# Where the scanned rows are asked for in the last stage of a four-layer image kernel

## The chip, the cores and the metric

The kernel runs on one core of one Trainium2 chip. The metric is the device time of one execution in microseconds (us). The profile comes from one further execution, taken by the hardware profiler on the same kernel.

## What is computed

The program applies four residual layers to 8 images of 256 x 256 x 64 floats. Only the last step of the last layer matters here. The fourth layer sees each image as a table of 4096 points with 256 channels; 1024 of these points are masked. For the masked points a sequential scan over the 1024 points gives new rows; these replace the old rows in the table, and the table is added to the image:

```python
def step(prev, inp):
    mn, bst, mx = inp
    ...
    cur = (d_ad[:, None] * prev + mx[:, None] * bst) / (d_ad + mx + EPS)[:, None]
    return (cur, cur)
_, gen = jax.lax.scan(step, jnp.zeros((b, c), x.dtype), xs)
out = feats.at[:, :, mask_point_idx].set(gen.transpose(1, 2, 0))
return out.reshape(b, c, h, w)
...
x = x + _L3_conv_ref(_gn(x), ...)
```

## The kernel before

The stages run one behind the other, each a block with its own programs for the five engines and a barrier at its end. The scan (`coherent_scan`) writes its rows to a tensor in device memory, `gen`, for all 8 images together; it ends at 14875 us of the profile. The change is in the stage behind it, the last one, `finish_points` (lines 2089 to 2180 or so). It goes through the images b = 0 to 7, and has five programs:

- SyncE (SP) issues all loads, in the order of its code, on one DMA queue (q1 in the profile). For each image: the scanned rows `g` (line 2116, 1024 rows of 1 KB, 1 MB in all), then the table of all points `f` (line 2120, 4096 rows of 1 KB, 4 MB), then the input `x` in two halves (line 2125, 2 MB each, runs of 8 KB). `g` has two buffers, used in turn, and so has `f`. Each half of `x` has one.
- GpSimd (POOL) writes the scanned rows of the image into the table `ft` in device memory, with eight indirect DMAs of 128 rows each (line 2133, queue q0). It waits for `g` of the image and for the row numbers.
- VectorE (DVE) makes the row numbers of the next image (lines 2158 to 2160). There is one set of them, so it first waits until the eight indirect DMAs of this image are done (semaphore `s_sc`). Then it makes 16 additions (line 2169), each of the transposed table in PSUM and a piece of `x`. Both are in this order in the code: the row numbers of image b+1 are written ahead of the additions of image b, behind those of image b-1.
- TensorE (PE) transposes the table, 64 blocks of 128 x 128 for an image (line 2147), once `f` has landed. It is ahead of the additions by at most four of the PSUM tiles.
- ScalarE (ACT) only issues the stores of the result, 2 MB for each half image (line 2178, queue q10), each once its eight additions are done.

SP's load of `f` for image b has to wait until the indirect DMAs of image b are done (they write what it reads), and for b of 2 and more until the table two images back is transposed. SP's load of a half of `x` waits for the eight additions of that half of the image before. The load of `g` for image b waits, from b = 2 on, for the indirect DMAs of image b-2, whose buffer it takes. Since SP works through its list in order, a wait in front of one load holds all later ones.

Of the kernel before, what the change touches and what calls it, by code (L numbers as in the profile page):

```python
# [14 lines left out]
P = 128  # L15
# [2073 lines left out]
def finish_points(nc, B, x3, ft, gen, mask_idx, eye, out):  # L2089

    TM, NT = NMASK // P, NPTS // P
    with ExitStack() as ctx:
        m = Mem(nc, ctx, "fp")
        g = m.sb("g", [P, 2, TM, H])
        f = m.sb("f", [P, 2, NT, H])
        x = m.sb("x", [P, 2, 2, NPTS // 2])
        o = m.sb("o", [P, 2, 2, NPTS // 2])
        idx0, idx, idxf = m.sb("idx0", [P, TM], I32), m.sb("idx", [P, TM], I32), m.sb("idxf", [P, TM])
        idn = m.sb("idn", [P, P])
        tp = [m.ps(f"tp{i}", [P, 2, 2, P]) for i in range(4)]  # L2100
        s_const, s_idx, s_ch = m.sem("const"), m.sem("idx"), m.sem("ch")
        s_g, s_f, s_x = ([m.sem(f"{n}{j}") for j in range(2)] for n in ("g", "f", "x"))
        s_sc, s_t, s_o = m.sem("sc"), m.sem("t"), m.sem("o")
        s_store = [m.sem(f"store{j}") for j in range(2)]
        ftf = ft.rearrange("b n h -> (b n) h")
        HT = NT // 2
        with nc.Block() as block:  # L2107

            @block.sync
            def _(sp):  # L2110
                sp.dma_start(idn[:, :], eye).then_inc(s_const, 16)  # L2111
                sp.dma_start(idx0[:, :], mask_idx.rearrange("(t p) -> p t", p=P), allow_slow_non_contiguous=True).then_inc(s_const, 16)  # L2112
                for b in range(B):
                    if b >= 2:
                        sp.wait_ge(s_sc, 16 * TM * (b - 1))
                    sp.dma_start(g[:, b % 2, :, :], gen[b].rearrange("(t p) h -> p t h", p=P)).then_inc(s_g[b % 2], 16)
                    sp.wait_ge(s_sc, 16 * TM * (b + 1))
                    if b >= 2:
                        sp.wait_ge(s_t, (b - 1) * HT)
                    sp.dma_start(f[:, b % 2, :, :], ft[b].rearrange("(t p) h -> p t h", p=P)).then_inc(s_f[b % 2], 16)  # L2120
                    for q in range(2):
                        if b:
                            sp.wait_ge(s_o, ((b - 1) * 2 + q + 1) * (HT // 2))
                        c0 = q * (NPTS // C // 2)
                        sp.dma_start(x[:, q, :, :], x3[b, :, c0:c0 + NPTS // C // 2, :].rearrange("(r p) w c -> p r (w c)", p=P)).then_inc(s_x[q], 16)  # L2125

            @block.gpsimd
            def _(pool):
                for b in range(B):
                    pool.wait_ge(s_g[b % 2], 16 * (b // 2 + 1))  # L2130
                    pool.wait_ge(s_idx, b + 1)
                    for i in range(TM):
                        pool.indirect_dma_start(ftf, bass.IndirectOffsetOnAxis(ap=idx[:, i:i + 1], axis=0),  # L2133
                                                g[:, b % 2, i, :], None).then_inc(s_sc, 16)

            @block.tensor
            def _(pe):
                pe.wait_ge(s_const, 32)
                for b in range(B):
                    pe.wait_ge(s_f[b % 2], 16 * (b // 2 + 1))  # L2140
                    for k in range(HT):
                        n = b * HT + k
                        if n >= 4:
                            pe.wait_ge(s_o, n - 3)
                        for r in range(2):
                            for i in range(2):
                                last = nc.tensor.transpose(tp[n % 4][:, r, i, :], f[:, b % 2, 2 * k + i, r * P:(r + 1) * P], idn[:, :])  # L2147
                        last.then_inc(s_t, 1)

            @block.vector  # L2150
            def _(dve):
                ch = Chain(dve, s_ch)
                dve.wait_ge(s_const, 32)
                ch.step(nc.vector.tensor_copy(idxf[:, :], idx0[:, :]))
                nc.vector.tensor_copy(idx[:, :], idxf[:, :]).then_inc(s_idx, 1)
                for b in range(B):
                    if b + 1 < B:
                        ch.step(nc.vector.tensor_scalar(idxf[:, :], idxf[:, :], float(NPTS), None, ALU.add))
                        dve.wait_ge(s_sc, 16 * TM * (b + 1))  # L2159
                        nc.vector.tensor_copy(idx[:, :], idxf[:, :]).then_inc(s_idx, 1)  # L2160
                    for k in range(HT):
                        n, q = b * HT + k, k // (HT // 2)
                        dve.wait_ge(s_t, n + 1)
                        if k % (HT // 2) == 0:
                            dve.wait_ge(s_x[q], 16 * (b + 1))
                            if b:
                                dve.wait_ge(s_store[q], 16 * b)  # L2167
                        c0 = (k % (HT // 2)) * 2 * P
                        nc.vector.tensor_tensor(o[:, q, :, c0:c0 + 2 * P], tp[n % 4][:, :, :, :].rearrange("p r i n -> p r (i n)"),  # L2169
                                                x[:, q, :, c0:c0 + 2 * P], ALU.add).then_inc(s_o, 1)  # L2170

            @block.scalar
            def _(act):
                for b in range(B):
                    for q in range(2):
                        act.wait_ge(s_o, (b * 2 + q + 1) * (HT // 2))
                        c0 = q * (NPTS // C // 2)
                        act.dma_start(out[b, :, c0:c0 + NPTS // C // 2, :].rearrange("(r p) w c -> p r (w c)", p=P),
                                      o[:, q, :, :]).then_inc(s_store[q], 16)
                for q in range(2):  # L2180
                    act.wait_ge(s_store[q], 16 * B)
# [671 lines left out]
```

## Time and profile before

| | us |
|---|---|
| median of 3 runs | 15209.85 |
| lowest and highest | 15209.34, 15213.14 |
| span of the profiled execution | 15214.5 |
| last stage in it, from its first load (14875) to the end | 339 |

The page of the profile gives the span from the first to the last instruction of one execution. No time around that span is given for this execution; the span itself is 4.65 us above the median of the three timed runs. Over the whole span TensorE's matrix work is busy 66%, VectorE 61%, ScalarE 52%, GpSimd 34%; the last 2.2% of the span, the stage of the change, is the part in which the DMA engines are busiest. To read it, one cuts this stage out of the trace: its chain of waits, the busy share and rate of the DMA engines in short stretches, and the share of each DMA queue.

### The profile page before, as it was taken

Reading aid. Unit: us, or ns where it says so; the run is one execution under the profiler, and the core shown is the slowest. Engines: PE = TensorE matmul, PEld = TensorE weight load, DVE = VectorE, ACT = ScalarE, POOL = GpSimd, SP = SyncE. Lnnn points to the kernel's source line nnn. Section 1 sums busy time; section 2 is a strip of 40 time slices with the busy share of each in tenths; the row PEclk is TensorE's granted clock in tenths of the full one; section 3 lists DMA queues with packets and bytes.
Section 4 is the critical chain, followed back from the end, with each engine's and each line's share of the span. In section 5 each row is a group of like instructions: output and inputs, shape, how many; then the busy total and the mean of one; then the engine's idle time right before and its main releaser. Section 6 shows DMA issues by size and latency. Waiting matters only on the chain. (4 is left out here: it accounts for less than half of the span.)

```text
span 15214.5 us, 295101 instructions
## 1 busy us (share of the span) xinstructions
PE 9980.4 (66%) x105986; PEld 7080.0 (47%) x105986; DVE 9300.2 (61%) x20130; ACT 7945.1 (52%) x14451; POOL 5137.7 (34%) x3844
## 2 busy tenths in 40 slices
PE   8655657999999998778777799866846770000002
PEld 3253223777777776666666688623223330000002
DVE  3213435777777777888888533225444547888882
ACT  5211223777777776566666422352334436777770
POOL 0003334556555555333333355300007891000001
PEclk9878878999999999999999999997878885555555
DMA  6787674111111111011111399978996661000008
GB/s 252 197 171 216 213 233 156 42 42 42 40 41 41 42 42 58 28 67 45 67 45 67 138 364 363 328 264 310 376 386 226 206 205 42 12 12 12 12 12 310
DMA packets 1245925, 2176.95 MB, mean 143 GB/s; under 512 B 99573, under 2 KB 900997, under 8 KB 1177605
## 3 DMA queue, kind: packets, MB, share of 16 engines
q1 hardware_dynamic: 813156, 1637.88, 32.9%
q10 hardware_dynamic: 410912, 463.54, 8.6%
q0 software_dynamic: 20608, 58.22, 1.5%
q8 instruction: 864, 14.16, 0.4%
q14 instruction: 385, 3.15, 0.1%
HBM read 1369.30 MB, written 790.14 MB: 142 GB/s over the span
## 5 line engine op out<-in xcount | busy, mean ns | idle before, releaser
L781 POOL TENSOR_TENSOR la_s<-la_s,la_mx 128x512 f32<-128x512 f32 x2048 | 2093.0, 1043 | 1462.7 <-DVE la_mx L740 1462.3
L2147 PE MATMUL fp_tp<-fp_idn,fp_f 128*128 128x128 f32 x512 | 89.6, 348 | 2547.0 <-DMA fp_f<-ft 2529.7
L820 ACT ACTIVATE la_et<-la_pt 128x512 f32<-128x512 f32 x2048 | 1119.0, 598 | 732.2 <-PE la_pt L652 732.1
L652 PE MATMUL la_pt<-la_idn,la_s 128*128 128x128 f32 x8192 | 1164.5, 287 | 220.5 <-POOL la_s L781 219.8
L2147 PEld LDWEIGHTS fp_tp<-fp_idn,fp_f 128*128 128x128 f32 x512 | 79.9, 184 | 2557.3 <-issue 2340.8
L740 DVE TENSOR_REDUCE la_mx<-la_s 128x16 f32<-128x1024 f32 x1024 | 1243.2, 1214 | 17.7
L732 DVE TENSOR_TENSOR la_s<-la_ps,la_post 128x2048 f32<-128x2048 f32 x512 | 1167.9, 2281 | 27.9 <-PE la_ps L638 27.7
L652 PEld LDWEIGHTS la_pt<-la_idn,la_s 128*128 128x128 f32 x8192 | 913.5, 145 | 334.2 <-issue 231.8
L1439 PE MATMUL pj_pp<-pj_pw,pj_at 128*128 128x256 f32 x4096 | 926.4, 379 | 0.0
L2133 POOL DMA_INDIRECT ft<-fp_g,fp_idx x64 | 62.2, 971 | 2503.4 <-DMA fp_g<-gen 2486.3
L956 PE MATMUL gm_xp<-gm_fws,gm_y 128*128 128x258 f32 x2048 | 559.7, 420 | 421.8 <-ACT gm_ri L1040 421.8
L1913 PE MATMUL sp_cp<-sp_tc 128*128 128x512 f32 x1536 | 697.1, 615 | 168.5 <-ACT sp_cos L1879 162.2
L1439 PEld LDWEIGHTS pj_pp<-pj_pw,pj_at 128*128 128x128 f32 x4096 | 758.3, 190 | 92.7
L1472 ACT ACTIVATE pj_at<-pj_tp 128x512 f32<-128x512 f32 x512 | 277.9, 594 | 861.0 <-PE pj_tp L1429 861.0
L2418 DVE SCALAR_TENSOR_TENSOR i_xo<-i_fp,i_xr 128x256 f32<-128x256 f32 x1024 | 379.8, 419 | 539.5 <-PE i_fp L2325 347.6
L1797 POOL DMA_INDIRECT sp_rows<-ft,sp_idx x256 | 242.8, 949 | 1339.6 <-DVE sp_idx L1922 1253.8
L1511 DVE TENSOR_TENSOR pj_o<-pj_pp,pj_xl 128x256 f32<-128x256 f32 x512 | 215.3, 420 | 753.1 <-PE pj_pp L1439 753.1
L956 PEld LDWEIGHTS gm_xp<-gm_fws,gm_y 128*128 128x128 f32 x2048 | 401.7, 206 | 563.5 <-issue 476.2
L2473 ACT ACTIVATE i_sq<-i_xo 128x4096 f32<-128x4096 f32 x64 | 231.5, 3617 | 814.4 <-issue 593.4
L1326 POOL TENSOR_TENSOR gm_sr<-gm_pc 128x512 f32<-128x512 f32 x64 | 70.0, 1093 | 1697.0 <-DVE gm_pc L1274 1697.0
L2440 POOL TENSOR_TENSOR i_acc<-i_acc,i_xo 128x4096 f32<-128x4096 f32 x56 | 496.3, 8862 | 410.9 <-DVE i_xo L2418 409.7
L751 DVE RECIPROCAL la_rc<-la_pt 128x32 f32<-128x32 f32 x512 | 183.2, 358 | 728.0 <-PE la_pt L661 728.0
(298 smaller groups left out, 28104.7 us busy)
## 6 DMA issues: line engine op xcount, KB each, us to landing
f_xt<-in_x SPq DMA_DIRECT2D x128, 1024.0 KB, 8.0
i_xr<-in_x SPq DMA_DIRECT2D x64, 2048.0 KB, 9.1
x<-pj_o SPq DMA_DIRECT2D x64, 2048.0 KB, 10.2
f_xt<-x SPq DMA_DIRECT2D x128, 1024.0 KB, 14.1
i_xr<-x SPq DMA_DIRECT2D x64, 2048.0 KB, 14.6
x<-i_xo ACTq DMA_DIRECT2D x64, 2048.0 KB, 14.5
sp_xt<-x SPq DMA_DIRECT2D x144, 512.0 KB, 4.6
out<-sp_xt SPq DMA_DIRECT2D x144, 512.0 KB, 2.9
```

The lines of the kernel that those rows point to most:

```text
L652: last = nc.tensor.transpose(t_bank(S, i)[:, h, :], s[:, S % RS, i, h, :], idn[:, :])
L732: nc.vector.tensor_tensor(s[:, S % RS].rearrange("p t h i -> p h t i"), ps[:, :, :, :, :, :].rearrange("p h g e d i -> p h (g e) (d i)"), ...
L740: nc.vector.reduce_max(mx[:, S % RS, ts, :].rearrange("p t h -> p (t h)"), s[:, S % RS, ts].rearrange("p t h (d i) -> p (t h d) i", d=2), ...
L781: nc.gpsimd.tensor_tensor(sv, sv, mb, ALU.subtract).then_inc(s_sub, 1)
L820: nc.scalar.activation(et[:, k % RT].rearrange("p h n -> p (h n)"), t_bank(S, i)[:, :, :].rearrange("p h n -> p (h n)"), ACT.Exp).then_inc ...
L956: last = nc.tensor.matmul(xp[c % 2][q][:, :], y[:, c % 2, wh, q * P:(q + 1) * P], fws[:, q, wh, :], start=(wh == 0), stop=(wh == 1))
L1439: last = nc.tensor.matmul(pp[gg // 2][:, gg % 2, :, :].rearrange("p w d -> p (w d)"), at[:, q, s, g * P:(g + 1) * P], pw[:, s, :, :].rearr ...
L1472: last = nc.scalar.activation(at[:, k % 2, s, :], tp[k % 2][s][:, :], ACT.Copy)
L1797: pool.indirect_dma_start(rows[:, b % 2, i, :], None, ftf, bass.IndirectOffsetOnAxis(ap=idx[:, i:i + 1], axis=0)).then_inc(s_g[b % 2][i // ...
L1913: last = nc.tensor.matmul(cp[n % 4][:, :], tc[:, r, i * P:(i + 1) * P], tc[:, r, c0:c0 + 512], start=(r == 0), stop=(r == 1))
L2418: last = nc.vector.scalar_tensor_tensor(halves(xo, j, r, i)[:, s], f[:, s], 0.0, x[:, s], ALU.max, ALU.add)
L2440: nc.gpsimd.tensor_tensor(acc[:, :], acc[:, :], xo[:, wc % 2, :], ALU.add).then_inc(s_acc, 1)
```

## The change

SP now issues the scanned rows of images 0 and 1 at once, directly behind the two small constants. Those of image b+2 are issued directly behind the table of image b, ahead of the two halves of the input. The wait in front of `g` is gone as a line of its own: the wait in front of the table of image b (all indirect DMAs up to image b done) stands ahead of it and covers it, since `g` of b+2 takes the buffer of `g` of b. No other engine's program is touched.

```diff
+                def rows(b):
+                    sp.dma_start(g[:, b % 2, :, :], gen[b].rearrange("(t p) h -> p t h", p=P)).then_inc(s_g[b % 2], 16)
+
+                rows(0)
+                rows(1)
                 for b in range(B):
-                    if b >= 2:
-                        sp.wait_ge(s_sc, 16 * TM * (b - 1))
-                    sp.dma_start(g[:, b % 2, :, :], gen[b].rearrange("(t p) h -> p t h", p=P)).then_inc(s_g[b % 2], 16)
                     sp.wait_ge(s_sc, 16 * TM * (b + 1))
                     if b >= 2:
                         sp.wait_ge(s_t, (b - 1) * HT)
                     sp.dma_start(f[:, b % 2, :, :], ft[b].rearrange("(t p) h -> p t h", p=P)).then_inc(s_f[b % 2], 16)
+                    if b + 2 < B:
+                        rows(b + 2)
                     for q in range(2):
```

At the start of the stage, SP's queue holds before (`fp_g` is the scanned rows, `fp_f` the table, `fp_x` the input, a closing x2 stands for two loads alike; the numbers behind L are lines of each kernel):

```order
1082 L2112 DMA fp_idx<-in_L_conv_mask_point_idx 128x8x1
1083 L2116 DMA fp_g<-gen 128x8x256
1084 L2120 DMA fp_f<-ft 128x32x256
1085 L2125 DMA fp_x<-x 128x2x2048 x2
1086 L2116 DMA fp_g<-gen 128x8x256
1087 L2120 DMA fp_f<-ft 128x32x256
1088 L2125 DMA fp_x<-x 128x2x2048 x2
```

The same place of SP's queue now:

```order
1082 L2112 DMA fp_idx<-in_L_conv_mask_point_idx 128x8x1
1083 L2114 DMA fp_g<-gen 128x8x256 x2
1084 L2122 DMA fp_f<-ft 128x32x256
1085 L2114 DMA fp_g<-gen 128x8x256
1086 L2129 DMA fp_x<-x 128x2x2048 x2
1087 L2122 DMA fp_f<-ft 128x32x256
1088 L2114 DMA fp_g<-gen 128x8x256
```

The rows of image 1 moved from behind the input of image 0 to in front of the table of image 0, and those of image 2 from behind the input of image 1 to in front of the input of image 0. At the end of the stage SP's queue holds before, for images 6 and 7:

```order
1101 L2116 DMA fp_g<-gen 128x8x256
1102 L2120 DMA fp_f<-ft 128x32x256
1103 L2125 DMA fp_x<-x 128x2x2048 x2
1104 L2116 DMA fp_g<-gen 128x8x256
1105 L2120 DMA fp_f<-ft 128x32x256
1106 L2125 DMA fp_x<-x 128x2x2048 x2
```

and now, for images 5 (its input) to 7:

```order
1101 L2129 DMA fp_x<-x 128x2x2048 x2
1102 L2122 DMA fp_f<-ft 128x32x256
1103 L2129 DMA fp_x<-x 128x2x2048 x2
1104 L2122 DMA fp_f<-ft 128x32x256
1105 L2129 DMA fp_x<-x 128x2x2048 x2
```

Between the input of image 6 and the table of image 7 no load stands any more.

## Rows read from the trace of the kernel before

**Rows 1.** Waits, 14800 to 15215 us: who waited for what, us, times, longest.
```profile
POOL ft L2133 <- DMA fp_g<-gen: 2486.3, 8, 2272.8
DVE fp_o L2169 <- DMA fp_x<-x: 170.8, 8, 30.3
...
SPq L2120 <- DMA ft<-fp_g,fp_idx: 223.2, 8, 29.8
```

**Rows 2.** Chain that ended last, one image: start us, duration us, what.
```profile
14893.17 0.37 SPq L2120
...
14893.58 8.62 SPq L2125
...
14903.46 17.76 DMA fp_g<-gen
...
14921.49 0.97 POOL ft L2133
...
14930.42 3.26 DMA ft<-fp_g,fp_idx
...
14933.69 0.37 SPq L2120
```

**Rows 3.** Stretches: length, busy of the engines, then TensorE clock, DMA share, GB/s.
```profile
14882.00:14893.00 11.00, 0.00 (x0) 0.00 (x0) 0.00 (x0) 0.00 (x0) 7.57 (x8) 0.50 0.27 95
...
14900.00:14905.00 5.00, 0.00 (x0) 0.00 (x0) 0.00 (x0) 0.00 (x0) 0.00 (x0) 0.50 1.10 348
14908.00:14913.00 5.00, 3.65 (x16) 3.28 (x16) 0.00 (x0) 0.00 (x0) 0.00 (x0) 0.50 1.01 419
...
14925.00:14930.00 5.00, 0.00 (x0) 0.00 (x0) 0.00 (x0) 0.00 (x0) 3.78 (x5) 0.50 1.01 398
14930.00:14935.00 5.00, 0.00 (x0) 0.00 (x0) 0.17 (x1) 0.00 (x0) 1.08 (x2) 0.50 0.64 216
14935.00:14940.00 5.00, 0.00 (x0) 0.00 (x0) 0.00 (x0) 0.00 (x0) 0.00 (x0) 0.50 1.00 335
...
15095.00:15100.00 5.00, 0.00 (x0) 0.00 (x0) 0.17 (x1) 0.00 (x0) 0.00 (x0) 0.50 0.64 195
...
15205.00:15210.00 5.00, 0.12 (x2) 0.00 (x0) 1.80 (x4) 0.00 (x0) 0.00 (x0) 0.80 1.01 418
14893.00:15201.00 308.00, 85.44 (x480) 76.34 (x481) 74.80 (x132) 0.00 (x0) 54.35 (x56) 0.61 0.98 361
8800.00:9600.00 800.00, 800.00 (x4438) 714.66 (x4437) 261.93 (x739) 199.98 (x369) 430.11 (x184) 1.00 1.05 363
...
11200.00:11400.00 200.00, 50.79 (x280) 46.10 (x278) 99.18 (x84) 46.79 (x69) 0.00 (x0) 0.61 1.03 412
```

**Rows 4.** DMA issues, 14870 to 15215 us: count, KB each, median us to landing.
```profile
fp_f<-ft SPq DMA_DIRECT2D x8, 4096.0 KB, 15.3
fp_x<-x SPq DMA_DIRECT2D x16, 2048.0 KB, 18.0
out<-fp_o ACTq DMA_DIRECT2D x16, 2048.0 KB
fp_g<-gen SPq DMA_DIRECT2D x8, 1024.0 KB, 17.8
ft<-fp_g,fp_idx POOLq DMA_INDIRECT x64, 4.6
```

**Rows 5.** DMA queues, 15045 to 15050 us: packets, MB, share of 16 engines.
```profile
q10 hardware_dynamic: 228, 1.74, 85.3%
q0 software_dynamic: 93, 0.26, 13.9%
```

**Rows 6.** Timeline: start us, duration us, engine, line, operation, count.
```profile
14881.76 1.00 POOL L2133 DMA_INDIRECT ft<-fp_g,fp_idx  x1 [2272.80 <-DMA fp_g<-gen]
...
15176.69 0.37 SPq L2120 DMA_DIRECT2D fp_f<-ft  x1
...
15201.32 5.47 DVE L2169 TENSOR_TENSOR fp_o<-fp_tp,fp_x 128x512 f32<-128x512 f32 x9 [0.16 <-PE fp_tp L2147]
```

## The prediction

> **What bounds the kernel now.** The change touches only the last stage, 339 us of 15214.5, so nothing outside it can move, and the most that the stage can give is small. I read it in this order. First the waits: GpSimd waits for the scanned rows before every image (the 2486.3 us hold 2272.8 us ahead of the stage, so 213.5 us fall inside it, over 8 images), VectorE waits 170.8 us for the input, and SP waits 223.2 us for the indirect DMAs before it may ask for a table [rows 1]. Every compute engine waits for data. Then the chain of one image: SP issues the table at 14893.17 and the first half of the input right behind, an issue that takes 8.62 us; then it asks for the rows of the next image at 14903.46, which take 17.76 us to land, because they stand in one queue behind 8 MB of table and input. Only then do the eight indirect DMAs start (14921.49), the last one is issued at 14930.42 and lands 3.26 us later, and at 14933.69 SP issues the next table [rows 2]. So by the chain the period of an image is issue, rows, indirect writes, issue: 14933.69 - 14893.17 = 40.5 us. The same period holds to the end: the eighth table is issued at 15176.69 [rows 6], and (15176.69 - 14893.17) / 7 = 40.50 us.
>
> Read alone, this chain promises far too much: 17.8 us of waiting for rows in each image would seem to go. The third view corrects it. The DMA engines are busy 0.98 of the time from 14893 to 15201, at 361 GB/s, and almost without a break: 1.10, 1.01, 1.01 in the stretches with table, input, and stores beside indirect writes; only where one image hands over to the next does the share fall, to 0.64 in 14930 to 14935, and to 0.64 in 15095 to 15100 [rows 3]. **The stage is bound by its bytes**; the chain is late only because its transfers stand behind other bytes that have to be moved anyway. What the change can take is the hole at the handover, plus what it moves into an idle time.
>
> **The size of the hole.** Two ways. By the share: 0.36 x 5 us = 1.8 us of full idleness in each of the two stretches named [rows 3]. That is a lower end, since the ramp on either side is cut off (the next stretch, 14935 to 14940, moves 335 GB/s instead of 348). By the bytes: an image moves 4096 KB of table, 1024 KB of rows and 1024 KB of indirect writes (8 x 128 rows of 1 KB), all in runs of 1 KB, and 4096 KB of input and 4096 KB of stores in runs of 8 KB [rows 4]. The 1 KB runs went at 348 GB/s (14900 to 14905), input alone at 419, stores alone at 418 [rows 3]. So 6.29 MB / 348 = 18.1 us and 8.39 MB / 418.5 = 20.0 us, together 38.1 us: the floor of a period. 40.5 - 38.1 = 2.4 us of hole. That the costs may be added like this shows in 14925 to 14930, where stores run beside indirect writes at 398 GB/s, between the two rates. I take 2.2 us, between the two ends.
>
> **The change part by part.** (a) Rows of image b+2 behind the table of image b, seven handovers. SP issues the same number of loads. Rows of image b+2 are in SBUF long before they are used. What then releases the indirect writes of b+2 is VectorE, whose row numbers come behind the additions of image b: the same moment in an image as now (the first is issued at 14921.49, [rows 2], as the additions end), but one image earlier for the same data. Let L be the time when the last half of input b lands. The additions end about 5 us later (nine of them took 5.47 us, [rows 6]); the indirect writes of b+2 run from L+5, and at today's pace (14921.49 to 14933.69, 12.2 us) end at about L+17. The table of b+2 has to stand in SP's queue before the bytes of image b+1 run out, at L+38.1. The slack is 21 us. The table of b+1 already stands behind the input of b when this lands, so at the handover there is work in the queue, and the hole goes: 7 x 2.2 = 15.4 us (ends 7 x 1.8 = 12.6 and 7 x 2.4 = 16.8). What is late next is nothing on an engine but the bytes, 38.1 to 38.3 us for an image. The input is pushed back by 1 MB of rows in its own image, 3.0 us at 348 GB/s, but the same 3.0 us no longer stand behind it, so the sum of bytes doesn't change; the first image shows it as a later addition, and no later one does.
>
> (b) Rows of image 1 ahead of the first table. They now move while the first eight indirect writes are being made, when the DMA engines are busy 0.27 of the time (14882 to 14893, [rows 3]). 1.05 MB / 348 = 3.0 us leave the saturated part. This cover has 11 x 0.73 = 8 us of room, so it is fully hidden. Indirect writes of image 1 likewise begin at about 14893 instead of 14921, but their bytes stay in the saturated part: nothing.
>
> (c) The rows of image 0 now share the engines with those of image 1. They are first in the same queue; at best they land as now, at worst all of the 3.0 us later. The queue takes requests in order ([rows 2]: rows behind 8 MB landed behind them), so I take 0.5 us, ends 0 and 3.0.
>
> (d) The removed wait and the order of buffers: nothing was queued on it, the wait of the table stands there already.
>
> (e) The tail. From the landing of the last input to the end nothing changes: nine additions from 15201.32, then the last store [rows 6]. Both kernels pay it.
>
> **Does mixing cost?** Before, table and input ran alone, and stores ran beside rows and indirect writes. Now stores of image b (8 KB runs on their own queue) run beside the table of b+1 (1 KB runs). No stretch of this stage shows that pair. The nearest rows: 8800 to 9600, loads and stores mixed in runs of mostly 1 KB, 363 GB/s; 11200 to 11400, stores in 1 KB runs beside loads in longer ones, 412 GB/s [rows 3]. With 363 for all 1 KB runs the period is 17.3 + 20.0 = 37.3 us, a further 0.8 us, 5 us in the stage; the other end is a loss of the same size. I take none, as the nearest row to this pair is the 398 of stores beside indirect writes.
>
> Sum: 15.4 + 3.0 - 0.5 = 17.9 us. On the profiled execution: 15214.5 - 17.9 = 15196.6. The median of the timed runs is 4.65 us below this span, so 15209.85 - 17.9 = **15192.0 us**.
>
> **How the queues share.** The one thing that is in danger is the pace of the indirect writes, which now meet two other queues. Beside stores they got 0.26 MB in 5 us, 52 GB/s, against 1.74 MB of stores [rows 5], though GpSimd issues 1 MB in about 10 us, some 100 GB/s; they caught up after the stores. So they are already held back by a queue of long runs. The Trainium skill says in "DMA: Bandwidth & Descriptors", section "Queues, rings and completion order", that each DMA engine serves its queues in turn, a packet at a time; by that rule the short packets get less than an equal share beside long ones, and the trace agrees in direction. The sum doesn't use the rule; the third rival is what it would do if it hit harder.
>
> **Rivals.**
> 1. Rates mix better than they add. 412 GB/s in 11200 to 11400 is for about a quarter of the bytes in 1 KB runs; if 1 KB runs went at 390 beside stores, the period would be 16.1 + 20.0 = 36.1 us, and the stage would gain 7 x 4.4 + 3.0 - 0.5 = 33 us: 15177. Against it: the stores take most of the engines while they last, and most of the table then runs alone, at 348. Chance 0.07.
> 2. The handover stays a bound, or the memory behind it does: a period of 40 us or a little more whatever the order, since the mean rate over an image can't rise above 361 GB/s [rows 3]. Then only part (b) and a remainder are left, 3 to 8 us: about 15204. For it: 363 GB/s in 8800 to 9600, with the DMA engines never idle. Against it: 419, 398 and 418 GB/s in stretches of this stage and 412 over 200 us elsewhere. Chance 0.11. The Trainium skill states in "DMA: Bandwidth & Descriptors", section "Specifications", a limit of about 358 GB/s from device memory for a core; by that 14.68 MB would need 41.0 us for an image, and the change would bring nothing. The trace speaks against that page, with 419 GB/s of input read from device memory.
> 3. Slower: indirect writes starved. In 15045 to 15050 they had 52 GB/s against one queue of 8 KB runs. If two such queues halved it to 26 GB/s for the whole of an image, 1.05 MB would take 40 us from L+5, the table of the next image but one would be issued at L+45 and begin about 1.7 us later: a period of 47 us, 6 us above today's for six images, less 3: about +33 us, 15243. It decides from the point at which the writes take more than 33 us (38.1 - 5); up to that they cost nothing. Against it: long runs of both queues meet only late in the period, when the input is under way; right behind the additions the load queue holds the table in 1 KB runs. Chance 0.04.
> 4. The change doesn't do what it says: some row load is still held, for instance because SP, in order, stands in the 8.62 us issue of an input [rows 2], and the table of b+1 comes into the queue too late in some images. It would leave half of the holes: gain 10 us, 15200, inside the range. Chance 0.08.
>
> **How the numbers follow.** The forecast (15183 to 15198) has 0.70. The range reaches from the gain with 1 KB runs at 363 and the larger hole, 7 x 3.2 + 3.0 = 25.4, and half of rival 1 (about 15178), to most of rival 2 (15205): 15178 to 15205. 0.2% of this time is 30.4 us, about what a measurement of this kernel can tell from no change. A gain of more needs a period under 36.6 us: only rival 1 with the upper end of everything, 0.06. A loss of more needs rival 3: 0.04. Within 0.2%: 0.90.
>
> **What would show it.** In the profile of the changed kernel: tables (line 2122) no longer one per 40.5 us but with inputs landing, and additions beginning, every 38 to 38.5 us; the DMA share at about 1.0 in every 5 us stretch from 14895 to about 15180, no stretch below 0.9; GpSimd waiting for VectorE's row numbers and no longer for rows, from image 2 on; the wait of SP for the indirect DMAs near zero from image 1 on, its time now in issues and in the wait for additions; the chain through table and input. Part (b) shows as a DMA share of about 0.5 instead of 0.27 in 14882 to 14893. Part (c) as the first indirect write later than 14881.76 [rows 6]. Wrong would be: 5 us stretches without holes but with a rate under 380 GB/s on the mean (rival 2), indirect writes that take over 30 us (rival 3), or a table issued after the input before it has landed (rival 4).

## The result

| | kernel before | changed kernel |
|---|---|---|
| median of 21 runs each, us | 15210.39 | 15181.89 |
| lowest and highest | 15199.65, 15224.01 | 15168.75, 15197.00 |
| span of the profiled execution | 15214.5 | 15167.1 |
| last stage in that profile, from its first load to the end | 339.3 | 310.8 |

The ratio is 0.9981, with a 95% interval of 0.9974 to 0.9987: 28.5 us less, 0.19%. The forecast was 17.9 us less (15192.0), range 15178 to 15205. Sign, range and the class "within 0.2%" held; the size was a third too small, and the inner interval of the forecast, 15183 to 15198, was missed by 1 us.

The profiled span alone would say 47 us. It must not be read so: the last stage begins at 14856.28 in the changed kernel and at 14875.17 before, though nothing ahead of it was touched. That is the spread of the earlier stages from execution to execution. The stage is what the change can move, and it became 339.33 - 310.82 = 28.5 us shorter, which is what the medians say. All experiments below are therefore compared by the length of the last stage.

**The profile after.** Stretches of the last stage of the changed kernel; the last three columns are TensorE's clock, the share of the DMA engines and GB/s:

```profile
14863.00:14874.00 11.00, 0.00 (x0) 0.00 (x0) 0.00 (x0) 0.00 (x0) 7.82 (x8) 0.50 0.45 155
14895.00:14900.00 5.00, 1.18 (x6) 0.77 (x4) 0.00 (x0) 0.00 (x0) 0.00 (x0) 0.84 1.01 423
14915.00:14920.00 5.00, 0.00 (x0) 0.00 (x0) 0.00 (x0) 0.00 (x0) 3.78 (x5) 0.50 1.04 431
14925.00:14930.00 5.00, 0.73 (x4) 0.73 (x5) 0.00 (x0) 0.00 (x0) 0.00 (x0) 0.50 1.10 368
14930.00:14935.00 5.00, 2.94 (x14) 2.54 (x12) 0.00 (x0) 0.00 (x0) 0.00 (x0) 0.50 1.05 425
...
14890.00:15150.00 260.00, 85.19 (x464) 79.72 (x464) 71.48 (x125) 0.00 (x0) 46.54 (x48) 0.61 1.05 400
```

The last line is the mean over most of the stage. The handover hole of [rows 3] is gone, and the mean rate rose from 361 to 400 GB/s. (The stage was not the part of the kernel with the busiest DMA engines, as the section on the profile before has it: 8800 to 9600 has a share of 1.05, this stage had 0.98 [rows 3].) The stretch of the first indirect writes, 0.27 before, is at 0.45: the rows of image 1 run there.

The waits in the same stage, by engine and then those of SP (us in all, times, longest):

```profile
POOL ft L2137 <- DMA fp_g<-gen: 2273.8, 1, 2273.8
DVE fp_o L2173 <- DMA fp_x<-x: 200.6, 8, 26.5
POOL ft L2137 <- DVE fp_idx L2164: 163.3, 7, 27.1
```

```profile
SPq L2129 <- DVE fp_o L2173: 37.9, 2, 20.2
...
SPq L2122 <- DMA ft<-fp_g,fp_idx: 19.5, 2, 16.4
```

Against [rows 1]: GpSimd waits for rows only before the first image, and then for VectorE's row numbers. SP waits 19.5 us for indirect writes, nearly all ahead of the first table, where it waited 223.2. VectorE waits for the input for longer than before, 200.6 us against 170.8, although the kernel is faster: the wait did not go, it became a wait for bytes alone.

One image in SP's queue, from its chain (start, duration; 2114 rows, 2129 input, 2122 table):

```profile
14890.36 0.70 SPq L2122
...
14891.11 31.37 SPq L2114
...
14922.52 3.58 SPq L2129
...
14926.14 0.82 SPq L2129
...
14927.08 0.54 SPq L2122
```

The tables of images 1 to 7 are issued from 14890.36 to 15110.84, so a period is 220.48 / 6 = 36.75 us, against 40.50 before and 38.3 in the forecast. The issue of the rows takes 31.37 us: table and rows now stand behind the input of the image before, and SP stands in the issue until 14922.48. That it waits there for room in its queue is inferred; no run tries it. It costs nothing, since the table issued at 14890.36 takes about 39 us to land (38.8 in the median), so SP is free about 7 us before the table has drained.

### The profile page after: what moved, and what is told of

It is laid out like the page before. It is cut to its first block and busy times, and to the rows that moved or that the text cites. A ratio compares the mean times of both kernels' runs of the same rounds, so it can differ in the third digit from the quotient of the medians.

```text
span 15167.1 us, 295101 instructions
## 1 busy us (share of the span) xinstructions
PE 9973.6 (66%) x105986; PEld 7082.3 (47%) x105986; DVE 9285.7 (61%) x20130; ACT 7946.3 (52%) x14451; POOL 5138.4 (34%) x3844
```

## The experiments

Each kernel is compared by its last stage. The stage repeats well: 339.3 and 339.2 us for the kernel before, 310.8 and 311.1 for the changed one (each in two profiles), while single total times moved by 10 us and more. The period is the time from the issue of the third table to that of the eighth, over 5; by it the kernel before has 40.4 and the changed one 36.8.

| kernel | stage, us | period, us | against |
|---|---|---|---|
| before, again | 339.2 | 40.5 | |
| rows of images 0 and 1 only | 333.1 | 40.6 | before: -6.2 |
| rows one image ahead | 331.1 | 39.3 | before: -8.1 |
| table on two queues (from before) | 369.8 | 44.2 | before: +30.6 |
| stores on the load queue | 312.8 | 37.2 | changed: +1.9 |
| rows in runs of 8 KB | 306.7 | 36.3 | changed: -4.3 |
| table and rows in long runs | 301.6 | 35.0 | changed: -9.3 |
| first input early | 304.4 | 36.2 | changed: -6.5 |
| long runs and early input | 297.7 | 35.0 | changed: -13.3 |
| table in runs of 4 KB | 303.8 | 35.1 | changed: -7.2 |
| 4 KB runs and early input | 302.8 | 35.1 | changed: -8.2 |
| changed, again | 311.1 | 36.6 | |

**The yardstick.**

> The kernel before once more. The last stage, from SP's first load in it to the end of the span, took 339.3 us in the profile before. Every theory here is about this stage alone; if its length is the same to 1 us while the whole span moves by several us, the stage length is the finer measure and the earlier stages are the noise. Expected: 338 to 341 us.

Measured: stage 339.2 us; total 15196.25 us, against 15206.82 for the same program beside it. The stage is the finer measure.

> The changed kernel once more, for the repeatability of its stage: 310.8 us in its profile; expected 310 to 312 us. If it comes out more than 1.5 us away, the differences of 2 us in the other runs say nothing.

Measured: 311.1 us. Differences of 2 us can be read.

**Part (b) alone.** In the changed kernel, the rows of later images go back behind the input:

```diff
                     sp.dma_start(f[:, b % 2, :, :], ft[b]...
-                    if b + 2 < B:
-                        rows(b + 2)
                     for q in range(2):
                         ...
+                    if 1 <= b < B - 1:
+                        rows(b + 1)
```

> Part (b) alone: the rows of images 0 and 1 are asked for at once, those of every later image stay behind the whole input of the image before (their old place). My sum: 3.0 us for the bytes moved into the idle time, and one handover (image 0 to 1) without a hole, 2.2 to 3.7 us; the other six periods stay at 40.5 us. Stage 333 to 335 us. Rival, that the early start of the first indirect writes is what speeds up the whole stage (a better phase between queues that then stays): later periods at 37 to 38 us and a stage under 322 us.

Measured: 333.1 us. Of the stage's 28.3 us (means of the two profiles of each kernel), 6.2 come from the start and the first handover; the other 22.1 us are six handovers of 3.7 us. So part (b) with (c) is 6.2 - 3.7 = 2.5 us, the forecast's 3.0 - 0.5, and the later periods are as before: an early start does not speed up the rest.

**One image ahead instead of two.**

```diff
                 rows(0)
-                rows(1)
...
-                    if b + 2 < B:
-                        rows(b + 2)
+                    if b + 1 < B:
+                        rows(b + 1)
```

> The rows of image b+1, not b+2, directly behind the table of image b; image 0 alone first. Theory that it is enough to have the rows before the handover: the rows land beside the table, about 20 us into a period, the indirect writes of b+1 take 12 to 15 us and are done by 35 us of 37: period 37 to 38, stage 312 to 320 us (310.8 plus 3 for the first rows). Rival, that indirect writes beside loads in 8 KB runs are slowed to 26 GB/s or so (1 MB in 40 us): the table of b+1 comes late, period over 42 us, stage over 345 us.

Measured: 331.1 us, period 39.3: between the two, and neither as it was put. The stretches at a handover of this kernel:

```profile
14990.00:14995.00 5.00, 5.00 (x29) 4.80 (x27) 3.32 (x7) 0.00 (x0) 2.71 (x3) 0.61 0.96 390
14998.00:15003.00 5.00, 0.04 (x1) 0.00 (x0) 1.97 (x5) 0.00 (x0) 0.00 (x0) 0.77 0.97 270
```

The first indirect write was issued at 14983.40, as the rows had landed, and the eight ran until 14995.59 beside the last input, and the table was issued just then, as the input had landed (14994.85). A hole stays, at 270 GB/s, partly filled by the store. The writes were not slowed to 26 GB/s: 12.2 us from the first issue to the next table, the same as before the change. The 40 us of my third rival do not come about; the rows simply came too late, 26.8 us into the period (14956.62 to 14983.40) and not the 20 of the expectation. That is what the second buffer of rows is for: two images ahead closes the hole, one does not.

**Is 348 GB/s a limit of one queue?** In the kernel before, the second half of each table is loaded from ACT's queue:

```diff
-                    sp.dma_start(f[:, b % 2, :, :], ft[b].rearrange(...)).then_inc(s_f[b % 2], 16)
+                    sp.dma_start(f[:, b % 2, :HT, :], ft[b, :NPTS // 2].rearrange(...)).then_inc(s_f[b % 2], 16)
...
             @block.tensor
-                    pe.wait_ge(s_f[b % 2], 16 * (b // 2 + 1))
+                    pe.wait_ge(s_f[b % 2], 32 * (b // 2 + 1))
...
             @block.scalar
                 for b in range(B):
+                    act.wait_ge(s_sc, 16 * TM * (b + 1))
+                    if b >= 2:
+                        act.wait_ge(s_t, (b - 1) * HT)
+                    act.dma_start(f[:, b % 2, HT:, :], ft[b, NPTS // 2:].rearrange(...)).then_inc(s_f[b % 2], 16)
```

> The kernel before, but the second half of each table is loaded from ACT's queue instead of SP's, at the same point. Same bytes, same runs of 1 KB, same waits. Theory that one queue of 1 KB runs by itself does not use the DMA engines fully (348 GB/s) and that a second queue beside it fills them: the table moves at 380 to 400 GB/s, 1.0 to 1.6 us less per image, stage 327 to 332 us. Rival, that 348 GB/s is what 1 KB runs cost in the engines whatever is beside them: stage 338 to 340 us.

Measured: 369.8 us, which neither theory gave. The rate is the rival's; the time is not, since both asked only for the rate. With both halves under way, first the stretch, then the two queues in it (packets, MB, share):

```profile
14886.00:14890.00 4.00, 0.00 (x0) 0.00 (x0) 0.00 (x0) 0.00 (x0) 0.00 (x0) 0.50 1.10 351
```

```profile
q1 hardware_dynamic: 684, 0.70, 55.5%
q10 hardware_dynamic: 686, 0.70, 54.4%
```

Two queues of 1 KB runs move 351 GB/s together, so 348 is no limit of a queue. The loss is another thing. Once SP's half is through, its input (8 KB runs, q1) stands against the other half table (1 KB runs, q10), here in 14890 to 14900:

```profile
q1 hardware_dynamic: 712, 3.31, 83.3%
q10 hardware_dynamic: 703, 0.72, 21.7%
```

Both queues get the same number of packets, and the half table moves at 72 GB/s. This is the first image, before any store is issued, so the half does not stand behind stores in ACT's queue. The issues of the whole stage, with the median us to landing:

```profile
fp_f<-ft SPq DMA_DIRECT2D x8, 2048.0 KB, 12.9
...
fp_f<-ft ACTq DMA_DIRECT2D x8, 2048.0 KB, 24.9
```

The half on ACT's queue lands 12 us later than SP's, the transposes wait for it, and with them the additions and the stores. In this run the queues shared by packets, not by bytes.

**Mixed or one behind the other.** In the changed kernel, the stores go to SP's queue:

```diff
                     for q in range(2):
                         if b:
                             sp.wait_ge(s_o, ((b - 1) * 2 + q + 1) * (HT // 2))
+                            store(b - 1, q)
                         ...
-            @block.scalar
-                (its 16 stores)
```

> The changed kernel, with the stores issued from SP's queue, each directly ahead of the input half that waits for the same additions, instead of from ACT's queue. Same bytes and waits; but packets of stores and of the table no longer alternate, they go one behind the other. It splits the surplus over my sum (period 36.8 us measured, 38.3 predicted). Theory that mixing the table's 1 KB loads with stores in 8 KB runs is cheaper than the two apart: the period rises to 37.4 to 38.1 us, the stage from 310.8 to 315 to 320 us. Rival, that mixing gives nothing and the whole surplus is a handover hole that was larger than I took (3.7 us, not 2.2): stage 310 to 312 us.

Measured: 312.8 us, period 37.2, 1.9 us for the stage: between the two, nearer the rival. Without any mixing of stores and table the period is still 0.9 us under my floor of 38.1. So the floor itself was wrong. Two stretches of this kernel, the table alone, and the end of the rows and then a store beside indirect writes:

```profile
14987.00:14995.00 8.00, 3.17 (x16) 2.46 (x16) 5.13 (x10) 0.00 (x0) 1.44 (x2) 0.62 1.10 349
15001.00:15008.00 7.00, 1.99 (x11) 1.75 (x9) 0.00 (x0) 0.00 (x0) 1.86 (x2) 0.74 1.02 424
```

The table still costs what I said (349). But indirect writes, which I had priced as 1 KB runs at 348, leave the rate at 424 here. The period says the same: no 5 us stretch of its periods has a share under 0.99, table and rows take 5.24 MB / 349 = 15.0 us of the 37.2, and input, stores and indirect writes, 9.44 MB, pass in the other 22.2 us, at 425 GB/s. In this kernel indirect writes cost no more than long runs. In the kernel before, stores on their own queue beside indirect writes had 398 [rows 3]; that difference is not explained.

**Are 1 KB load runs what costs?** In the changed kernel, each partition gets eight rows that lie together, with the row numbers to match:

```diff
-mask_idx.rearrange("(t p) -> p t", p=P), allow_slow_non_contiguous=True
+mask_idx.rearrange("(p t) -> p t", p=P)
-gen[b].rearrange("(t p) h -> p t h", p=P)
+gen[b].rearrange("(p t) h -> p t h", p=P)
```

> The changed kernel with only the scanned rows in runs of 8 KB (and their row numbers laid out to match); table and additions as they are. It prices 1 KB load runs without the slow additions that spoiled the runs with a long table. Theory that a byte in a 1 KB load run costs 1/348 and else 1/422: 1.05 MB x (1/348 - 1/422) = 0.53 us per image, 6 images in the saturated part and a little at the start: stage 310.9 - 3 to 4 = 307 to 308 us, periods of 36.2 to 36.3 us. Rival, that the rows, small and beside stores or indirect writes, already cost no more than long runs: stage 310.5 to 311.5 us.

Measured: 306.7 us, period 36.3; 4.3 us less, a little over the 3 to 4 of the theory: 6 x 0.53 = 3.2 by the theory, and the first table is issued 17.4 us into the stage instead of 18.4. The same for the table, whose points then have to be put back in order by the additions:

```diff
-sp.dma_start(f[:, b % 2, :, :], ft[b].rearrange("(t p) h -> p t h", p=P))
+sp.dma_start(f[:, b % 2, :, :].rearrange("p (s t) h -> p s t h", s=2), ft[b].rearrange("(s p t) h -> p s t h", s=2, p=P))
...
+t0 = (k % (HT // 2)) * 2
+cols = [v[:, q, :, :].rearrange("p r (n t) -> p r t n", t=HT)[:, :, t0:t0 + 2, :] for v in (o, x)]
+nc.vector.tensor_tensor(cols[0], tp[n % 4][:, :, :, :], cols[1], ALU.add)
```

> The changed kernel with other layouts in SBUF: table and scanned rows are loaded with a partition's rows next to each other in device memory (table: 16 rows, 16 KB, for each half; scanned rows: 8 rows, 8 KB), and the additions read and write their columns 64 bytes apart to put the points back. Theory that 348 GB/s is the price of 1 KB runs: 5.24 MB per image at 418 instead of 348 GB/s saves up to 2.5 us per image, less where the table already runs beside stores: stage 292 to 298 us. Rival, that the additions with 64-byte steps become slower and the bound (16 of them over 1.4 us each, where the halves land 5 us apart): stage over 310 us, with additions above 680 ns. Rival two, that device memory and not the run length holds the table at 348: stage 309 to 312 us.

Measured: 301.6 us. The run length is the cause of the 348: with nothing of these loads changed but their layout, table, rows and stores now go at over 420 (one stretch). But the additions take longer (duration min, median, max in ns):

```profile
14980.00:14990.00 10.00, 4.63 (x29) 2.94 (x28) 9.79 (x13) 0.00 (x0) 0.00 (x0) 0.99 0.99 422
```

```profile
L2174 DVE TENSOR_TENSOR fp_o<-fp_tp,fp_x x128: 992/1064/1205, 14903.5 to 15156.5; 128x512 f32<-128x512 f32 x128
```

680 ns became 1064. This is not the bound in every period, but each image's stores and the next input now come up to 16 x 0.38 = 6 us later. 9.3 us of the 13 to 19 expected came. Most of the rest stands at the end of the stage, where nothing covers the additions. The last 16 of them, in the changed kernel (to the end of its span at 15167.1) and in this one (15165.1):

```profile
15149.74 9.81 DVE L2173 TENSOR_TENSOR fp_o<-fp_tp,fp_x 128x512 f32<-128x512 f32 x16 [20.88 <-DMA fp_x<-x]
```

```profile
15142.35 15.28 DVE L2174 TENSOR_TENSOR fp_o<-fp_tp,fp_x 128x512 f32<-128x512 f32 x16 [17.92 <-DMA fp_x<-x]
```

From their start to the end it takes 22.8 us instead of 17.4, 5.4 us more, and 9.3 + 5.4 = 14.7 us is inside what was expected. What the slow additions cost within the periods was not tried apart.

> As the kernel with long runs, but the table comes in runs of 4 KB (4 rows for a partition), so the additions step 16 bytes instead of 64. Theory that the 64-byte steps made the additions slow (1064 ns against 680) and that this gave back part of the gain (later stores and inputs): additions at 680 to 800 ns, periods of 34.5 to 35.3 us against 35.9, stage 293 to 298 us. Rival, that any step slows them alike: 1.06 us, stage 301 us again. Rival two, that runs of 4 KB are still short: table rates between 348 and 420 GB/s, stage 298 to 305 us.

The step and the run length of the table both changed (`t=4` in place of 16 rows). Measured: 303.8 us, additions 1076 ns. For the additions the first rival holds: steps of 16 and of 64 bytes cost alike. The stage is 2.2 us over the 301 of that rival and inside the 298 to 305 of the second. A stretch of 2 us with the table in 4 KB runs alone (14936 to 14938) goes at 418 GB/s, so these runs are hardly short; where the 2.2 us are was not settled.

**The first input early.** In the changed kernel:

```diff
                 rows(0)
                 rows(1)
+                half(0, 0)
+                half(0, 1)
                 for b in range(B):
...
-                    for q in range(2):
-                        if b:
-                            sp.wait_ge(s_o, ...)
+                    if b:
+                        for q in range(2):
+                            sp.wait_ge(s_o, ...)
```

> The changed kernel, with both input halves of image 0 asked for directly behind the rows of images 0 and 1, ahead of the wait for the indirect writes and the first table. 4.19 MB / 418 = 10.0 us leave the saturated part for the stretch in which the first indirect writes are made. Theory that this time is free: 7 to 10 us less, stage 301 to 304 us. Rival, that the first eight indirect writes, on which the first table waits, are slowed by packets of 8 KB beside them (in the kernel before they moved 52 GB/s beside stores instead of 100): they end 5 to 10 us later, stage 306 to 311 us.

Measured: 304.4 us, 6.5 us less. The first table is issued 21.6 us into the stage (14885.13 - 14863.49) instead of 18.4: the indirect writes pay 3.2 us for the 10.0 us that leave the rest. 10.0 - 3.2 = 6.8, close to what was measured. Both effects were there, and the first is larger.

**Faster than both.**

> Both edits of the two kernels before this one together, timed. If both gains hold and add: stage 283 to 292 us, 19 to 28 us less than the changed kernel and 47 to 56 us less than the kernel before, ratio 0.9963 to 0.9969. If the additions are slowed into the bound: ratio above 0.998.

Measured: stage 297.7 us; 15156.29 us against 15203.33 beside it, ratio 0.9968, interval 0.9955 to 0.9980. The gains do not add in full (9.3 + 6.5 = 15.8, 13.3 measured), and the stage is above the expected 283 to 292, while the ratio is inside the expected range; the additions took 1056 ns here too. By the stage it is the fastest kernel tried, 41.6 us under the kernel before.

> The same with both input halves of image 0 asked for early, timed. If the gains add, as 6.4 us did for the early input alone: stage 286 to 292 us, 47 to 53 us less than the kernel before, ratio 0.9965 to 0.9970. With the rival of slow additions: stage 297 us, ratio about 0.9972.

Measured: stage 302.8 us, ratio 0.9975, interval 0.9964 to 0.9985. Here the early input brought 1.0 us, not 6.5, and neither expectation was met. Part of it shows in the rates: in 14910 to 14920 they fall to 343 and 288 GB/s, where the kernel with runs of 4 KB alone shows no stretch under 398 between 14885 and 15105. Against 424 this is 2.6 us. What opens this hole, and where the rest is, was not settled.

## Why the prediction was right in kind and short in size

**What bounds the stage: right.** 17.8 us of waiting for rows in every image was worth 3.7 us, because the bytes behind the wait had to be moved anyway. The wait for the input even grew. The size was 10.6 us short. That the time still lies in the range is in part luck: its lower end, 15178, was reached with half of rival 1, which is not what happened; with the forecast's own terms alone, 25.4 us, it would have been 15184.5.

**(a) Seven handovers of 2.2 us: the term that was mis-sized.** It measured 3.7 us (36.75 against 40.50), so 26 us instead of 15.4. Two steps of it failed.

- The hole was read too small. I took 5 x 0.36 = 1.8 us from the DMA share in 14930 to 14935 [rows 3]. The same row has 216 GB/s, where about 400 were to be had: 5 x (1 - 216 / 400) = 2.3 us, and 0.2 us in the next row. A handover later, in the kernel before:

```profile
14970.00:14975.00 5.00, 0.00 (x0) 0.00 (x0) 0.17 (x1) 0.00 (x0) 1.95 (x2) 0.50 0.68 246
14975.00:14980.00 5.00, 0.00 (x0) 0.00 (x0) 0.00 (x0) 0.00 (x0) 0.00 (x0) 0.50 0.87 278
```

  By the rate this is 5 x (1 - 246 / 400) + 5 x (1 - 278 / 348) = 1.9 + 1.0 = 2.9 us. Two things were missed. A full share is not 1.00 here but 1.01 with long runs and 1.10 with the table alone [rows 3], so that 0.87 while the table alone is loaded is a gap of a fifth. And the hole reaches into the next 5 us, where a share of 1.00 looked full at 335 of 348 GB/s. I called 1.8 a lower end but then let it pull the estimate down from 2.4.
- The floor of 38.1 us was too high, since all 1 KB pieces were priced at 348. With indirect writes at 422 it is 0.5 us less, with input and stores at 424 instead of 418.5 another 0.3: 37.3. The kernel with the stores on the load queue, which has no hole, measured 37.2. So 40.5 - 37.2 = 3.3 us of the 3.7 come without any mixing of stores and table, and the rest is what their alternation gives: 0.4 us by the periods, 1.9 / 7 = 0.3 by the stage, from one run. The forecast set that last term at zero between a gain and a loss of 0.8; it was a gain of 0.3 to 0.4. Of the 3.3 us, the rates of two handovers account for 2.5 and 2.9; the 398 of stores beside indirect writes before, against 424, would be a source of the rest, but no run tries it.

**(b) and (c): right.** 2.5 us together against 3.0 - 0.5. From SP's issue of the first rows to the first indirect write it took 5.71 us before and 6.15 after (14857.16 to 14863.31), 0.4 us later for the 0.5 assumed.

**(d) and (e): right.** New waits stand where the old one was, GpSimd's 163.3 us for row numbers and SP's 37.9 us for additions, but none opens a gap: from 14880 to 15150 no 5 us stretch has a share under 1.00. The tail is unchanged: from the start of the last 16 additions to the end it took 17.6 us before (15196.86 to 15214.5) and 17.4 after (15149.74 to 15167.1).

**Rival 1 (better mixing)** had the nearest period of the rivals, 36.1 us, and a nearer time than the forecast, 15177, for the wrong reason: 1 KB loads did not become faster beside stores by much (0.3 to 0.4 us for an image). Nearer still was the far end of my own terms, a larger hole and 1 KB runs at 363 together, a gain of 25.4 us. **Rival 2** is refuted: 400 GB/s on the mean over 260 us, 431 in a stretch of loads, stores and indirect writes. The limit of about 358 GB/s of the Trainium skill ("DMA: Bandwidth & Descriptors", "Specifications") did not bind this core, which ran alone; the measurement decides. **Rival 3**: the indirect writes took a median of 6.3 us from issue to landing instead of 4.6 [rows 4], but behind the first table SP waited for them only once, 3.1 us before the last one, with the input of the image before still on its way; the slack of 21 us was never used up. **Rival 4** did not occur: each table was issued behind the input of the image before, ahead of its landing.

**What the profile was to show**: a share of 1.0 throughout, GpSimd on VectorE's row numbers, SP's wait nearly gone, all as put, and a share of 0.45 for the 0.5 of part (b); the period of 38 to 38.5 us was the one mark missed.

## What to carry to other kernels

When a chain of waits runs through a stage whose DMA engines are nearly always busy, price a prefetch by the bytes per second that are missing in the gaps, and not by the waits that it removes. If the busy share is used, compare it with its value in a full stretch of the same transfers, here 1.01 to 1.10, and look at the stretches on both sides. How far ahead to fetch follows from the slot in which the fetched data is used: here one image ahead was worth 8 us and two were worth 28. And do not put short runs that are needed next on a queue of their own beside a busy queue of long runs: a half table in 1 KB runs against an input in 8 KB runs landed 12 us late. Where nothing waits for the short runs, as with the table beside the stores in the changed kernel, the separate queues did no harm (310.8 us, against 312.8 with both on one).

## What the runs showed of the hardware

- Busy queues take turns by packets. In the changed kernel, with stores (q10), table (q1) and, in the second stretch, indirect writes (q0) under way (14985 to 14990 and 14991 to 14994; packets, MB, share):

```profile
q10 hardware_dynamic: 238, 1.82, 86.3%
q1 hardware_dynamic: 238, 0.24, 13.7%
```

```profile
q10 hardware_dynamic: 106, 0.87, 68.2%
q0 software_dynamic: 107, 0.31, 25.4%
q1 hardware_dynamic: 105, 0.11, 10.1%
```

  The packet counts are equal, and the bytes stand as 7.6 to 1. The rule of the Trainium skill ("DMA: Bandwidth & Descriptors", "Queues, rings and completion order"), that an engine serves its queues in turn, a packet at a time, fits these counts.
- Loads in 1 KB runs went at 348 to 351 GB/s, on one queue and on two; input in 8 KB runs at 419 [rows 3]; table and rows in 16 and 8 KB runs, with stores beside them, at 422. Indirect writes of 1 KB rows beside a store left the rate at 398 in the kernel before [rows 3] and at 424 with the store on the load queue. Their packets are larger than a row, 0.31 MB in 107 packets.
- An addition of 128 x 512 took 680 ns with neighbouring columns and 1056 to 1076 ns with columns 16 or 64 bytes apart.
